# Two-quarter steps, a numerator in two 64-row halves, and 1024-column VectorE operations in an attention and LoRA-expert kernel

## The reference

```python
# attention, 8 images of C=512 channels by N=2048; 8 heads of 64
qh = softmax(layernorm(x) as (B, N, H, dh), axis=dh)
kh = softmax(ctx as (B, N, H, dh), axis=N)
kvs = einsum('bnhd,bnhe->bhde', kh, vh)        # vh is ctx too
x = x + einsum('bnhd,bhde->bnhe', qh, kvs)
# feed-forward: LoRA experts, the 2 best of 4, on layernorm(x) per row
logits = flat @ router_w.T
gates = softmax(top 2 of logits)
mid = einsum('tf,erf->ter', flat, A)
x = x + einsum('te,teo->to', gates, einsum('ter,eor->teo', mid, B) * 4.0)
```

## Time and profile before

| | |
|---|---|
| median of 3 runs | 462.5 us (462.09 to 462.72) |
| profiled execution | 461.86 us, its span 460.1 us |
| PE busy | 434.0 us (94%) |
| DVE busy | 378.9 us (82%) |
| POOL busy | 358.7 us (78%) |
| ACT busy | 317.8 us (69%) |
| moved by DMA | 137.55 MB, mean 299 GB/s |

### The profile page before, as it was taken

The page is one execution under the profiler, slowest core; times in us unless marked ns, Lnnn a source line. Parts: engine busy times, 40 slices in busy tenths (PEclk is TensorE's granted clock), DMA queues, the critical chain, the costliest instruction groups (busy, mean ns, idle before and its releaser), DMA issues.

```text
span 460.1 us, 16033 instructions
## 1 busy us (share of the span) xinstructions
PE 434.0 (94%) x6504; PEld 382.7 (83%) x6504; DVE 378.9 (82%) x1045; ACT 317.8 (69%) x436; POOL 358.7 (78%) x343
## 2 busy tenths in 40 slices
PE   6569998999999999999999999999999999999975
PEld 5458887888889888888888988888888988888854
DVE  2478778898998989898988989898989989775864
ACT  1266888795858777786858777786958687785320
POOL 0457999988898989898898988898888989894510
PEclk9658999999999999999999999999999999999997
DMA  8995997799999999999999999999999997445247
GB/s 288 420 410 187 310 274 266 261 285 322 347 285 355 327 342 345 312 336 320 339 305 323 338 361 334 323 326 328 355 291 345 300 366 256 172 170 184 93 182 275
DMA packets 38969, 137.55 MB, mean 299 GB/s; under 512 B 4208, under 2 KB 6384, under 8 KB 38768
## 3 DMA queue, kind: packets, MB, share of 16 engines
q1 hardware_dynamic: 38896, 136.52, 85.8%
HBM read 102.95 MB, written 33.55 MB: 297 GB/s over the span
## 4 chain that ended last, share of the span: by engine, by line
PE 80%; POOL 6%; DVE 4%; DMA 4%; issue 2%; ACT 2%; SPq 1%; POOLq 0%; DVEq 0%
PE num_ps L407 23%; PE kv_ps L390 15%; PE raw_ps L423 12%; PE delta_ps L478 11%; PE delta_ps L479 6%; PE kv_ps L438 5%; PE raw_ps L454 4%; DMA sq_a<-in_bt_dram 4%; POOL ek_sb L311 3%; POOL y_sb L323 3%; PE kv_ps L443 1%; PE raw_ps L464 1%; DVE max_n L632 1%; DVE y_sb L716 1%; PE kv_ps L375 1%
## 5 line engine op out<-in xcount | busy, mean ns | idle before, releaser
L311 POOL TENSOR_TENSOR ek_sb<-ctx_sb,kmax_row 128x512 f32<-128x512 f32 x128 | 167.6, 1311 | 35.7 <-ACT kmax_row L511 35.7
L323 POOL TENSOR_TENSOR y_sb<-attnT,y_sb 128x512 f32<-128x512 f32 x128 | 164.0, 1281 | 38.6 <-DVE attnT L707 38.5
L407 PE MATMUL num_ps<-kv_sb,x_sb 128*128 128x130 f32 x1024 | 140.8, 281 | 3.3 <-ACT kv_sb L563 2.0
L407 PEld LDWEIGHTS num_ps<-kv_sb,x_sb 128*128 128x128 f32 x1024 | 125.7, 192 | 6.2 <-ACT kv_sb L563 2.7
L716 DVE TENSOR_TENSOR y_sb<-delta_ps,y_sb 128x512 f32<-128x512 f32 x128 | 87.5, 684 | 23.3 <-PE delta_ps L479 22.1
L632 DVE TENSOR_REDUCE max_n<-ctx_sb 128x32 f32<-128x512 f32 x128 | 86.4, 677 | 10.6 <-DMA ctx_sb<-in_ctxt_dram 10.6
L390 PE MATMUL kv_ps<-ctx_sb,ek_sb 128*64 128x65 f32 x2048 | 93.2, 234 | 0.2 <-ACT ek_sb L533 0.2
L707 DVE TENSOR_TENSOR attnT<-num_ps,rden 128x512 f32<-128x512 f32 x128 | 88.5, 691 | 4.8 <-DVE rden L704 0.4
L390 PEld LDWEIGHTS kv_ps<-ctx_sb,ek_sb 128*64 128x64 f32 x2048 | 74.6, 140 | 17.8 <-issue 6.0
L533 ACT ACTIVATE ek_sb<-ek_sb 128x1024 f32<-128x1024 f32 x64 | 67.2, 1049 | 25.8 <-POOL ek_sb L311 25.7
L423 PE MATMUL raw_ps<-w_sb,y_sb 128*64 128x69 f32 x2048 | 84.4, 223 | 0.0
(11 more groups left out here) (67 smaller groups left out, 461.7 us busy)
## 6 DMA issues: line engine op xcount, KB each, us to landing
ctx_sb<-in_ctxt_dram SPq DMA_DIRECT2D x64, 520.0 KB, 5.6
x_sb<-in_x_dram SPq DMA_DIRECT2D x64, 512.0 KB, 6.1
y_sb<-in_xt_dram SPq DMA_DIRECT2D x64, 512.0 KB, 6.5
out_dram<-y_sb SPq DMA_DIRECT2D x60, 512.0 KB, 6.3
out_dram<-y_sb SPq DMA_DIRECT2D x8, 256.0 KB, 3.8
sq_a<-in_bt_dram SPq DMA_DIRECT2D x1, 1024.0 KB, 16.2
w_sb<-in_wt_dram SPq DMA_DIRECT2D x1, 552.0 KB, 10.1
cst<-in_consts_dram SPq DMA_DIRECT2D x1, 145.0 KB, 2.3
```

The costliest lines, as they stand in the source:

```text
L311: pool.tensor_tensor(ek_sb[:, t % 2, chunks(g), :].rearrange("p (a b) c -> p a b c", b=2), ctx_sb[:, t % 4, 2 * g:2 * g + 2, 1:P + 1, :].r ...
L323: pool.tensor_tensor(y, attnT[:, g, :], y, ALU.add).then_inc(x1_made, 1)
L407: mm = pe.matmul(num_ps[:, j // 2, at:at + 2 * (DH + 1)], x_sb[:, t % 4, c * P:(c + 1) * P], kv_sb[:, t % 2, :], start=True, stop=True, sk ...
```

## The change

- All compute engines take two quarters a step: the loops run over every second q, from -10 to 4 NT + 20. SP's loop did so already.
- PE's `numerator` makes each chunk in two matmuls with a stationary operand of 128x64, into the two partition halves of `num_ps`. Both numerators of a step stand together with two `kv` and two `project`; the deltas of both quarters stand ahead of them.
- `delta_ps` becomes one tensor of two banks. DVE's `add_delta` adds 1024 columns once for both quarters, and the deltas of a step wait for the addition of the step before. `max_ps` moves from `num_ps` to the first bank of `delta_ps`, so that the first delta of a step also waits for `kmax` when one is due.
- `max_part` takes 64 output columns from 1024 inputs, once a step.
- `fold_squares` folds all 16 chunks into one block of 128 columns with 16 matmuls of 128 columns; `copy_squares` copies 128 columns, `sum_squares` is one matmul.
- DVE's order in a step becomes `kv_recip`, `max_whole`, `add_delta`, `normalise`, `mid_low`, `max_part`, `normalise`, then the gates, `bn_part` twice, and the small operations of the layer norm. The gates' two halves stand at the ends of two neighbouring steps.
- B's high part is made in ACT's step q = 2 instead of 0 and its low part in DVE's step 4 instead of 0 to 3. The last pair is stored in 4 pieces instead of 8.

```diff
-                after(pe, attn_made, 4 * (t - 3) + 3)
+                pe.wait_ge(max_made, 2 * t + 2)
+                after(pe, out_made, adds_until(4 * t - 4))
                 pe.transpose(max_ps, max_n[:, t % 2, :], ident).then_inc(maxT_done, 1)
...
-                    pe.wait_ge(kmax_made, min(t + 3, NT))
...
-                    mm = pe.matmul(num_ps[:, j // 2, at:at + 2 * (DH + 1)], x_sb[:, t % 4, c * P:(c + 1) * P],
-                                   kv_sb[:, t % 2, :], start=True, stop=True, skip_group_check=True)
+                    for half in range(2):
+                        n = slice(half * DH, (half + 1) * DH)
+                        c = (g * CH + j) * P + half * DH
+                        mm = pe.matmul(num_ps[n, j // 2, at:at + 2 * (DH + 1)], x_sb[:, t % 4, c:c + DH],
+                                       kv_sb[:, t % 2, :], start=True, stop=True, skip_group_check=True)
...
+                for k in range(NCH // 4):
+                    for s in range(4):
+                        sq = sq_b if k >= 2 else sq_a[:, t % 2, :]
+                        at = (4 * k + s) % 8 * P
+                        mm = pe.matmul(kv_ps[(t + 1) % 2][32 * s:32 * s + 32, 2 * P:3 * P], ones[:, 0:32],
+                                       sq[:, at:at + P], start=(k == 0), stop=(k == 3), skip_group_check=True)
...
-                after(pe, out_made, 8 * p + i - 1)
+                if i % 2 == 0:
+                    after(pe, out_made, 4 * p + i // 2)
+                    after(pe, kmax_made, min((8 * p + i + 22) // 4 + 2, NT))
...
-            for q in range(FIRST, LAST + 1):
+            for q in range(FIRST, LAST + 1, 2):
                 delta(*delta_at(q))
+                delta(*delta_at(q + 1))
+                sum_squares(tile_in(q, 12))
+                turn_mid(pair_in(q, 20))
+                if q == 2:
                     sum_w()
+                spread_kmax(tile_in(q, -4))
+                numerator(*tile_at(q, 6))
+                for k in range(2):
+                    kv(*tile_at(q + k, 0))
+                project(*tile_at(q, 8))
+                numerator(*tile_at(q + 1, 6))
+                project(*tile_at(q + 1, 8))
+                turn_max(tile_in(q, -6))
+                fold_squares(tile_in(q, 10))
...
-                dve.wait_ge(delta_done, 8 * p + i + 1)
-                y = y_sb[:, pair_slots(p), 2 * i:2 * i + 2, :]
-                dve.tensor_tensor(y, delta_ps[i % 2][:].rearrange("p (j t c) -> p t j c", j=2, t=2), y,
+                dve.wait_ge(delta_done, 8 * p + i + 2)
+                y = y_sb[:, pair_slots(p), 2 * i:2 * i + 4, :]
+                dve.tensor_tensor(y, delta_ps[:].rearrange("p b (j t c) -> p t (b j) c", j=2, t=2), y,
                                   ALU.add).then_inc(out_made, 1)
...
+            for q in range(FIRST, LAST + 1, 2):
+                a, b = pair_in(q, 16), pair_in(q, 18)
+                kv_recip(tile_in(q, 4))
+                max_whole(tile_in(q, -4))
+                ln1_mean(tile_in(q, -2))
+                add_delta(*delta_at(q))
                 if b is not None:
+                    gate_rank(b)
+                normalise(*tile_at(q, 6))
+                mid_low(pair_in(q, 20))
                 max_part(*tile_at(q, -8))
+                normalise(*tile_at(q + 1, 6))
                 if a is not None:
                     gate_centre(a)
...
                     gate_logits(a)
                     gate_below(a)
+                    gate_beats(a, 0)
+                    gate_beats(a, 1)
+                    gate_mask(a)
                 if b is not None:
                     gate_select(b)
                     gate_sum(b)
                     gate_scale(b)
+                    gate_mid(b)
+                for k in range(2):
+                    bn_part(*tile_at(q + k, -4))
+                ln1_var(tile_in(q, 0))
+                ln1_bias(tile_in(q, 2))
```

More of the change, by code:

```diff
@@ L120, in xattn_lora_moe_kernel @@
         num_ps = bank("num_ps", (P, 2, 512))
-        delta_ps = [bank("delta_ps0"), bank("delta_ps1")]
-        max_ps = num_ps[:, 0, 3 * P:4 * P]
+        delta_ps = bank("delta_ps", (P, 2, 512))
+        max_ps = delta_ps[:, 0, 0:P]
         ctx_landed = [sem(f"ctx_landed{i}") for i in range(4)]
@@ L199, in tile_at, with tile_in, pair_in, adds_until @@
             return (t, g) if 0 <= t < NT else (None, g)
-        def pair_at(q, offset):
-            p, r = divmod(q - 4 - offset, 8)
+        def tile_in(q, offset):
+            t, g = divmod(q - offset, 4)
+            return t if g == 0 and 0 <= t < NT else None
+        def pair_in(q, offset):
+            p, r = divmod(q - offset, 8)
             return p if r == 0 and 0 <= p < NP else None
         def delta_at(q):
-            p, i = divmod(q - 21, 8)
+            p, i = divmod(q - 22, 8)
             return (p, i) if 0 <= p < NP else (None, i)
+        def adds_until(q):
+            return max(0, min((q - 22) // 2, 4 * NP))
         def chunks(g):
@@ L286, in _ @@
                 if 2 <= t < NT:
-                    after(sp, raw_done, quarters_done(q, 7))
+                    after(sp, raw_done, quarters_done(q, 8))
                     if t >= 8:
@@ L294, in _ @@
                     load_ctx(t, r // STEP)
-            for i in range(8):
-                sp.wait_ge(out_made, 8 * (NP - 1) + i + 1)
+            for i in range(4):
+                sp.wait_ge(out_made, 4 * (NP - 1) + i + 1)
                 store_last(i)
@@ L433, in fold_squares, with sum_squares @@
                 after(pe, row_made, min(t + 4, NT))
[L434 to L444, removed]
+                for k in range(NCH // 4):
[4 more added lines that the diff above has]
+                                       sq[:, at:at + P], start=(k == 0), stop=(k == 3), skip_group_check=True)
                 mm.then_inc(sq_folded, 1)
-            def sum_squares(q):
-                t, g = tile_at(q, 12)
-                if t is None or g:
+            def sum_squares(t):
+                if t is None:
                     return
@@ L452, in sum_squares, with turn_mid @@
                 pe.wait_ge(sq_summed, t + 1)
[L453 to L459, removed]
+                pe.matmul(raw_ps[p % 2][:, odd, COL_SQ:COL_SQ + 2], sq_sum[:, t % 2, :], ones[:, 0:2],
+                          start=False, stop=True, skip_group_check=True).then_inc(sq_done, 1)
+            def turn_mid(p):
                 if p is None:
@@ L685, in ln1_bias, with kv_recip @@
                                       ALU.mult).then_inc(nbias1_made, 1)
-            def kv_recip(q):
-                t, g = tile_at(q, 4)
-                if t is None or g:
+            def kv_recip(t):
+                if t is None:
                     return
@@ L798, in gate_mid, with mid_low @@
                         ALU.mult).then_inc(mid_made, 1)
-            def mid_low(q):
-                p = pair_at(q, 16)
+            def mid_low(p):
                 if p is None:
```

160 lines of the change are left out of this document (56 added, 104 removed).

## The result

The changed kernel takes 506.47 us (median of 6 runs, 502.78 to 510.44) against 462.47 us (6 runs, 461.86 to 462.72) of the kernel before: a ratio of 1.0943, 95% interval 1.0896 to 1.099. The prediction had the direction, and about a third of the size: +13.5 us instead of +44.

What follows compares the result with a forecast made beforehand. It took PE to bound the kernel before, and PE and DVE alternating afterwards: 14 periods x 1.14 = +16 us, start -2, end 0, so span 460.1 becomes 474, time 476 us; range 464 to 496.

Steps and rivals of the forecast that it cites:

- The wait for `kmax`: In every second step PE's deltas wait for DVE's max_whole: PE stands still 1.1 to 1.3 us, twice a pair.
- Rival 1: PE stays the bound and the kernel gets faster, about 23.5 us a pair and 430 us in all; chance 0.12.
- The period: In the steady part a pair of tiles takes 26.8 us instead of 25.66, as PE and DVE alternate.
- C and D: Last two of a pair's four steps, with mid_low and four bn_part in place of the gates: 13.3 us together.
- A and B: First two of a pair's four steps, with the gates, counted from the end of max_whole: 13.5 us together.
- The transfers aren't pressed either: DMA: 332 GB/s on average, 419 in bursts, and a longer period asks for less.
- The numerator's halves: The two 64-wide halves overlap on PE, so eight double records take 0.89 us again.
- rival 2: The numerator's halves run one after the other: 33.4 us a pair, 570 us in all; chance 0.05.
- The mode changes: PE's round trips between 64-wide and 128-wide operands fall from eight to four a pair, 0.37 us each: 1.5 us less.
- Rival 3: TensorE's clock drops in the waits: 1.8 us more a pair, about 500 us in all; chance 0.07.
- The start: Near the start, B's load two to four quarters later holds up less: -2 us, bounds 0 and -5.
- The end: Last pair: additions and deltas alternate, but four instead of eight, and a larger store ends last: 0, bounds -1 and +3.

Runs made afterwards that it cites:

- both reductions early: The changed kernel with DVE's kv_recip and max_whole moved to the step before, right behind the second normalise: 488.56 us, 1.0525 of the kernel before.
- Small stores: The changed kernel with both reductions early, each store of a finished tile cut to one chunk of eight (except the last pair): 465.19 us, 1.0078.
- the whole numerator: The changed kernel with both reductions early and the numerator again one 128x128 matmul a chunk: 471.67 us, 1.0201 of the kernel before.
- `kmax` early: The changed kernel with only max_whole moved to the step before, behind the second normalise: 497.42 us, 1.0735 of the kernel before.
- the set-up early: The changed kernel with the sums of the weights and B's high part in step 0, its low part in steps 0 and 2: 500.54 us, 1.0818.
- everything mended: The changed kernel with both reductions early, the set-up early, the numerator whole and two additions of 512 columns: 462.85 us, 1.0025 of the kernel before.

## Why the prediction was right in direction and wrong in size

- **The wait for `kmax`: right.** It stands where it was put, twice a pair; 1.27 and 1.49 us instead of 1.1 and 1.3, and DVE's own wait behind it is 1.37 where about 1.4 was forecast. Rival 1, PE as the bound, fell with it. With both reductions early the clean pair is 24.8 us, of which PE waits 0.8 for `attnT`: about 24.0 of its own, where the prediction had added up 23.5.
- **The period: the mechanism right, the term mis-sized.** "26.8 us a pair instead of 25.66" was 27.5. C and D took 13.78 instead of 13.3, A and B 13.71 instead of 13.5. The count had 0.05 for PE to wake after `kmax`, and the chain has 0.14; it had 1.05 from the end of a `normalise` to the end of the numerator that waits for it (9.35 to 10.4), and the chain has 1.18 (309.95 to 311.13). `mid_low` and the reciprocal behind `max_part` start 0.72 and 1.25 us after the operation ahead of them, not 0.61 and 1.13. The upper bound of 28, "0.05 more at every semaphore", was the right kind of doubt. (Two sums of the range don't come out: 23.5 and twice 1.2 is 25.9, not 26.1, and 28 us a pair gives 493 us, not 495.) 1.81 to 1.84 instead of 1.14 a pair: 8.1 us over the 12 pairs in the middle.
- **"The transfers aren't pressed either": the step that failed.** It asked only whether a transfer would come late, and put the added instructions at nothing. The share of the DMA engines was 0.96, and what else goes through them is PE's instructions: 18731 instead of 16033 in all. In the profiled execution that cost 11.6 us in the steady part, the largest of four terms that were missed (the sum below); without it the time would have been near 495 to 499 us, so no single term explains the miss. Small stores (longest gap 3.5 to 0.99 us) and the whole numerator (3.5 to 1.36 us) each shorten the gaps, two independent ways.
- **The numerator's halves: right** as to their overlap (0.89 to 0.92 without a wait ahead, 16 records), so rival 2 is out. That they cost PE nothing else was wrong, see the step above.
- **The mode changes: right in the rows, not in the time.** 0.15 to 0.17 us a change is what both orders show, and the Trainium skill, page "TensorEngine Tiling (Array Packing)", section "Tiling Modes", agrees in kind; but the 1.5 us a pair lie in a stretch where PE waits anyway. With the waits gone, halves give a clean pair of 24.8 against 25.1 with the numerator whole.
- **Rival 3, the clock: seen, but as a consequence.** It falls behind the gaps and stays at 1.00 through the regular waits of 1.27 and 1.49 us, as "against it" had said. In this execution it made each gap dearer; in others some gaps leave it as it was (with `kmax` early, those of 1.44, 1.62 and 2.01 us).
- **The start: wrong sign.** -2 was predicted, +4.5 measured (+2.7 by `kmax` of tile 4, 57.7 against 55.0). The sum had looked at when B's load lets DVE go, and not at `sum_w`, 7 us of PE in step 2 (20.37 to 27.4), now ahead of the second of two `kv`, for whose end DVE's reciprocal waits 7.02 us. That this wait is the cause isn't shown: with the set-up early, `kmax` of tile 7 starts at 96.3 as before. It starts at 88.5 and 89.8 in the two kernels that have the set-up early together with both reductions early and two additions.
- **The end: wrong.** 0 with a bound of +3 was predicted, +10.4 measured. The "additions and deltas of the last pair alternate instead of overlapping" was seen and priced at nothing. The chain's end after:

```profile
498.40 0.58 PE delta_ps L476
...
500.26 0.23 PE delta_ps L477
...
500.51 1.24 DVE y_sb L709
501.75 0.04 issue
501.79 0.58 PE delta_ps L476
```

  One round is 3.4 us for 1024 columns. The rounds at 482.8 and 485.2 took 2.5 each, with deltas of 0.12 and PE idle for 1.3 in each; from 487.5 on the granted clock is 0.50 (1.2 GHz), and a delta takes 0.21. From the first delta of the last pair to the end of the last addition pass 13.5 us, where before it were 7.6 (447.6 to 455.3, are from it). With two additions it is 7.6 again in the kernel with everything mended, so this loss is the handing over of both banks at once. 5.9 of the 10.4 us are here; two more pairs at 1.8 each would be 3.7 of the rest, which was not taken apart further.

Together, against the forecast span of 474: the middle had 12 x 1.14 = 13.7 us and lost 33.4, so +8.1 for the period and +11.6 for the gaps with the slower clock behind them; the start +6.5; the end, where two pairs at 1.14 had been allowed, +8.1. That is 34.3, and 508.4 less 474 is 34.4.

## What to carry to other kernels

Where one engine fills the chain and a second stands 10% behind it, look at the order of the second as soon as the first gets faster: the squares alone gave 1%, and moving one operation that nobody waits for gave 2% on top. (That move was not run without the squares.) Doubling the step's size, which shares a bank between the two engines, cost 9% with all that came with it, and was no gain with every loss that was found taken out.

Before splitting a matmul for the sake of modes, count its instructions. The mean share of the DMA engines is no measure of the risk by itself: from 100 to 400 us it was 0.95 in the kernel before, without a gap, and 0.88 in the kernel after, with four. What the trace does show is idle time inside a group that has no wait, with a packet of the instruction queue that starts late. At a pipeline's end price each handover by itself, with the clock that an engine has which idles in between.

## What the runs showed of the hardware that was not expected

- PE can run dry. In the kernel after, gaps of 1.4 to 2.6 us with no releaser, three of four in the middle of a matmul group, came where the DMA engines were at their full share and a packet of 16 KB of the instruction queue had just started. With both reductions early and the same instructions, the longest gap was 3.5 us at a share of 0.95 over the steady part, and 0.99 at 0.80.
- The traces show what it waits for. Number PE's instructions in order of time from 0, with weight loads, matmuls and waits: in the 13 traces there are 50 gaps without a releaser of 0.5 us or more, and the first instruction behind every one of them has the number 193 plus a multiple of 256. The instruction queue q8 moves about one packet of 16 KB for each 256 of them (52 for 13273 before, 62 for 16103 after). So the gaps stand only where PE passes from one packet's instructions to the next.
- The packets start late; they don't take long. PE goes on 2.2 to 2.5 us after such a packet's start in all 50 cases, and the packets themselves took 0.88 to 1.04 us, as most others do. From a packet's start to PE's first instruction out of it pass never under 2.17 us in any trace. Between 60 and 400 us the median of it is 5.7 us in the kernel before (least 3.2), 4.1 in the kernel before with halves, 3.8 in the kernel after, 2.7 with both reductions early, and from there 4.0 with small stores and 3.6 with the numerator whole. Less data and fewer instructions both give the packets time. What decides when a packet starts stays open: the kernel before with halves has a share of 0.97 from 100 to 400 us and 60 packets, and no gap over 0.99.
- The first delta behind a wait for DVE starts 0.14 us after `kmax` ends, and a numerator group behind a wait takes 1.11 to 1.13 us against 0.89 to 0.92 without.
- An addition of 1024 float32 columns takes 1.22 us and a maximum 1.21, as estimated from the rows of 128 and 512.
